# Attention of the latent feed-forward block: values of two head pairs at once on four 32-column tiles, one output bank, three banks in turn for the transposes

## The reference, cut to what matters

```python
ckv = x @ Wkva
kv_latent, k_rope = (ckv[:, :, :R], ckv[:, :, R:])            # R = 16
kv = (kv_latent @ Wkvb).reshape(b, t, H, NOPE).transpose(0, 2, 1, 3)
q = jnp.concatenate([q_nope, _rope(q_rope)], axis=-1)
k = jnp.concatenate([kv, _rope(k_rope)], axis=-1)
v = jnp.concatenate([kv, jnp.zeros_like(k_rope)], axis=-1)
att = jnp.einsum('bhqd,bhkd->bhqk', q, k) / jnp.sqrt(jnp.float32(D))
mask = jnp.tril(jnp.ones((t, t), dtype=bool))
att = jnp.where(mask, att, jnp.float32(-jnp.inf))
att = jax.nn.softmax(att, axis=-1)
y = jnp.einsum('bhqk,bhkd->bhqd', att, v)
return y.transpose(0, 2, 1, 3).reshape(b, t, H * D) @ Wo
```

## Time and profile before

| what | value |
| --- | --- |
| median of 3 runs | 2208.24 us (2206.58 to 2211.63) |
| the profiled execution | 2207.7 us |
| its span in the profile | 2205.9 us |
| loop of `attention_2f`, first scores to last values, each of four | 75.1 us (first: 459.3 to 534.4) |
| PE busy over the span | 1917.1 us, 87% |
| DVE, ACT, POOL busy | 55%, 42%, 36% |
| mean granted TensorE clock | 0.925 of full speed |

### The profile page before, as it was taken

One profiled execution on the slowest core, in us unless ns is written; L12 is line 12 of the kernel. 1 busy time (PEld: TensorE's weight loads), 2 busy tenths in 40 slices (PEclk: granted clock), 3 DMA queues, 4 the chain that ended last, 5 costly groups with the idle time before them and its releaser, 6 DMA issues. The chain is left out here.

```text
span 2205.9 us, 32131 instructions
## 1 busy us (share of the span) xinstructions
PE 1917.1 (87%) x11205; PEld 1234.1 (56%) x11205; DVE 1217.5 (55%) x3078; ACT 925.5 (42%) x2062; POOL 797.5 (36%) x959
## 2 busy tenths in 40 slices
PE   3369799898969989989896999989897998979989
PEld 3236556555655646656574655656574565646655
DVE  4336746455476636546386645646466464654544
ACT  0025355344543436527353336526453552542221
POOL 0124536454351116545252014635343453530000
PEclk9569899999989999989897999999898999999999
DMA  5120000001102000000203000000200000030030
GB/s 188 45 84 1 0 1 1 1 1 32 47 16 107 1 5 1 1 1 1 77 1 122 1 5 1 1 1 1 78 1 1 1 1 1 1 111 5 2 118 5
DMA packets 32303, 59.08 MB, mean 27 GB/s; under 512 B 6160, under 2 KB 10512, under 8 KB 30992
## 3 DMA queue, kind: packets, MB, share of 16 engines
q1 hardware_dynamic: 32144, 57.03, 7.3%
HBM read 53.86 MB, written 3.16 MB: 26 GB/s over the span
## 5 line engine op out<-in xcount | busy, mean ns | idle before, releaser
L1213 POOL TENSOR_TENSOR rows<-rows,rinv 128x512 f32<-128x512 f32 x256 | 260.7, 1039 | 311.2 <-DVE rinv L1398 311.2
L1393 DVE TENSOR_REDUCE nmax<-psum 128x2 f32<-128x1088 f32 x128 | 165.1, 1290 | 124.4 <-PE psum L1263 124.4
L1354 ACT ACTIVATE rows<-psum,nmax 128x544 f32<-128x544 f32 x256 | 180.3, 709 | 52.0 <-DVE nmax L1393 52.0
L1988 ACT ACTIVATE region_b<-psum 128x512 f32<-128x512 f32 x132 | 78.8, 597 | 256.4 <-PE psum L1933 256.3
L2029 DVE TENSOR_TENSOR region_b<-region_b,psum 128x512 f32<-128x512 f32 x128 | 87.9, 686 | 160.9 <-PE psum L1957 154.0
L1273 PE MATMUL psum<-weights,rows 128*128 128x128 f32 x1024 | 162.5, 281 | 7.2 <-ACT turned L1361 3.7
L1257 PE MATMUL psum<-region_a,region_b 64*128 64x256 f32 x1024 | 160.2, 404 | 9.7 <-ACT rows L1354 5.9
L1957 PEld LDWEIGHTS psum<-region_c,region_b 128*128 128x128 f32 x1024 | 133.7, 192 | 47.6 <-issue 27.9
L1273 PEld LDWEIGHTS psum<-weights,rows 128*128 128x128 f32 x1024 | 114.8, 148 | 58.7 <-issue 58.7
L1291 PE MATMUL psum<-turned,region_a 128*64 128x256 f32 x1024 | 137.9, 391 | 3.8 <-DVE turned L1404 3.5
L1404 DVE COPY turned<-psum 128x512 f32<-128x512 f32 x128 | 88.5, 691 | 87.9 <-PE psum L1273 87.7
(11 more groups left out here) (468 smaller groups left out, 3804.3 us busy)
## 6 DMA issues: line engine op xcount, KB each, us to landing
region_a<-w_centred SPq DMA_DIRECT2D x32, 258.0 KB, 5.3
region_a<-in_w SPq DMA_DIRECT2D x32, 256.0 KB, 4.6
region_a<-in_eg SPq DMA_DIRECT2D x32, 256.0 KB, 5.7
region_a<-in_eu SPq DMA_DIRECT2D x32, 256.0 KB, 5.9
region_c<-in_weights SPq DMA_DIRECT2D x32, 256.0 KB, 6.7
weights<-in_weights SPq DMA_DIRECT2D x4, 1264.5 KB, 9.3
w_centred<-region_a SPq DMA_DIRECT2D x1, 2064.0 KB, 6.3
region_a<-in_w SPq DMA_DIRECT2D x1, 2048.0 KB, 22.3
```

The source lines that it names most:

```text
L1213: nc.gpsimd.tensor_tensor(row, row, rinv[:, 2 * u + j:2 * u + j + 1].broadcast_to([P, S]), ALU.mult).then_inc(done, 1)
L1354: nc.scalar.activation(heads_of(u, j), scores_of(u, j), ACT.Exp, bias=nmax[:, 2 * u + j:2 * u + j + 1], accum_out=psum_of[:, 2 * u + j:2 * ...
L1393: nc.vector.tensor_reduce(nmax[:, 2 * u:2 * u + 2], both_scores(u), AX.X, ALU.max, negate=True).then_inc(s.mx, 1)
```

## The change

`values` works on a group of two pairs: for each of the four key blocks it issues four products (two pairs, two heads), each on a 32-column tile of its own, so that all four column tiles of the array have work. It runs at the steps 11, 19, 27 and 35 instead of 7, 11, 15, ..., 35, four times in place of eight, with the same number of matmuls altogether. All groups write bank 7 and each waits for the copy of the group before it. Bank 6, now free, joins 4 and 5: transposes take the three in turn. The transposed rows of three pairs are kept instead of two; the third pair's lie in the unused halves of `region_c` (first head) and `turned` (second head).

```diff
+            def turned_head(p, j):
+                if p % 3 < 2:
+                    return turned_f[:, 2 * (p % 3) + j, :, :]
+                return part(region_c if j == 0 else turned, T * S, [P, T, S])
+
             def turned_to(u, j):
-                p, t = u // T, u % T
-                return turned_f[:, 2 * (p % 2) + j, 0:t + 1, P * t:P * (t + 1)]
-
-            def o_bank(p):
-                return bank(6 + p // 2 % 2)
+                t = u % T
+                return turned_head(u // T, j)[:, 0:t + 1, P * t:P * (t + 1)]
+
+            def turn_bank(u, j):
+                return bank(4 + (2 * u + j) % 3)
...
                     def turn(u, j):
                         pe.wait_ge(s.pn, u + 1)
-                        if u >= 1:
-                            pe.wait_ge(s.ca if j == 0 else s.cb, u)
+                        if j == 0 and u >= 2:
+                            pe.wait_ge(s.cb, u - 1)
+                        if j == 1 and u >= 1:
+                            pe.wait_ge(s.ca, u)
                         for k in range(u % T + 1):
-                            mm = nc.tensor.transpose(bank(4 + j)[:, P * k:P * (k + 1)], rows_of(u)[:, j, P * k:P * (k + 1)],
+                            mm = nc.tensor.transpose(turn_bank(u, j)[:, P * k:P * (k + 1)], rows_of(u)[:, j, P * k:P * (k + 1)],
                                                      ident[:, :])
...
-                    def values(p):
-                        pe.wait_ge(s.ca, T * (p + 1))
-                        pe.wait_ge(s.cb, T * (p + 1))
-                        if p >= 4 and p % 2 == 0:
-                            pe.wait_ge(s.on, p // 2 - 1)
+                    def values(g):
+                        pe.wait_ge(s.ca, 2 * T * (g + 1))
+                        pe.wait_ge(s.cb, 2 * T * (g + 1))
+                        if g >= 1:
+                            pe.wait_ge(s.on, g)
                         for k in range(T):
-                            for j in range(2):
-                                lo = 2 * LAT * (2 * (p % 2) + j)
-                                mm = nc.tensor.matmul(o_bank(p)[lo:lo + 2 * LAT, P * k:S], latv[:, k, :],
-                                                      turned_f[:, 2 * (p % 2) + j, k, P * k:S],
+                            for n in range(4):
+                                lo = 2 * LAT * n
+                                mm = nc.tensor.matmul(bank(7)[lo:lo + 2 * LAT, P * k:S], latv[:, k, :],
+                                                      turned_head(2 * g + n // 2, n % 2)[:, k, P * k:S],
                                                       start=(k == 0), stop=(k == T - 1), skip_group_check=True)
                         mm.then_inc(s.o, 1)
...
-                        if step >= 7 and step % T == 3:
-                            values(step // T - 1)
+                        if step >= 11 and step % (2 * T) == 3:
+                            values(step // (2 * T) - 1)
...
                     def copy_first(u):
                         act.wait_ge(s.ta, u + 1)
-                        if u >= 2 * T:
-                            act.wait_ge(s.o, u // T - 1)
+                        if u >= 3 * T:
+                            act.wait_ge(s.o, (u // T - 3) // 2 + 1)
...
                     def copy_heads(g):
-                        act.wait_ge(s.o, 2 * (g + 1))
-                        nc.scalar.activation(aot[:, g, :], bank(6 + g % 2), ACT.Copy).then_inc(s.on, 1)
+                        act.wait_ge(s.o, g + 1)
+                        nc.scalar.activation(aot[:, g, :], bank(7), ACT.Copy).then_inc(s.on, 1)
...
                     def copy_second(u):
                         dve.wait_ge(s.tb, u + 1)
-                        if u >= 2 * T:
-                            dve.wait_ge(s.o, u // T - 1)
+                        if u >= 3 * T:
+                            dve.wait_ge(s.o, (u // T - 3) // 2 + 1)
```

More of the change, by code:

```diff
@@ L1580, in copy_first @@
                         act.wait_ge(s.ta, u + 1)
-                        if u >= 2 * T:
-                            act.wait_ge(s.o, u // T - 1)
-                        nc.scalar.activation(turned_to(u, 0), bank(4)[:, 0:keys(u)].rearrange("p (k q) -> p k q", q=P),
+                        if u >= 3 * T:
+                            act.wait_ge(s.o, (u // T - 3) // 2 + 1)
+                        nc.scalar.activation(turned_to(u, 0), turn_bank(u, 0)[:, 0:keys(u)].rearrange("p (k q) -> p k q", q=P),
                                              ACT.Copy).then_inc(s.ca, 1)
                     def copy_heads(g):
-                        act.wait_ge(s.o, 2 * (g + 1))
-                        nc.scalar.activation(aot[:, g, :], bank(6 + g % 2), ACT.Copy).then_inc(s.on, 1)
+                        act.wait_ge(s.o, g + 1)
+                        nc.scalar.activation(aot[:, g, :], bank(7), ACT.Copy).then_inc(s.on, 1)
                     for step in range(units + 4):
@@ L1620, in copy_second @@
                         dve.wait_ge(s.tb, u + 1)
-                        if u >= 2 * T:
-                            dve.wait_ge(s.o, u // T - 1)
-                        nc.vector.tensor_copy(turned_to(u, 1), bank(5)[:, 0:keys(u)].rearrange("p (k q) -> p k q", q=P)).then_inc(s.cb, 1)
+                        if u >= 3 * T:
+                            dve.wait_ge(s.o, (u // T - 3) // 2 + 1)
+                        nc.vector.tensor_copy(turned_to(u, 1), turn_bank(u, 1)[:, 0:keys(u)].rearrange("p (k q) -> p k q", q=P)).then_inc(s.cb, 1)
                     for step in range(units + LAG + 1):
```

## The result

The changed kernel takes 2228.84 us (median of 4 runs, 2226.4 to 2233.4) against 2209.59 (2206.58 to 2211.63): a ratio of 1.0091, 95% interval 1.0070 to 1.0112, 19 to 20 us slower. The forecast was 2229.

What follows compares the result with a forecast made beforehand. The prediction took alternating ACT and DVE work, 8.32 us a pair, as the bound, not PE. Terms -0.2 + 3.0 + 2.7 = +5.5 us an execution, +22 for four, on 2207.7, put at 2229 us; range 2206 to 2242.

Steps and rivals of the forecast that it cites:

- ACT and DVE are the bound, PE is as long beside them: Loop of attention_2f: ACT and DVE take turns, 8.32 us a pair; PE takes 8.34 but does not set the pace.
- the ring: Loop of attention_2f: row maximum (DVE), exponentials (ACT), reciprocals (DVE), next maximum, each waiting for the last; 8.32 us a pair.
- Four tiles run side by side: Values on PE: a group of two pairs takes 2.28 instead of 4.56 us, freeing 9.1 us of PE an execution.
- The tiles-in-turn rival: Values on PE: third and fourth tile run after the first two, 4.56 us a group, +36 us, 2243; chance 0.09.
- The head's 0.2 us: Start of the loop: the first values move away and the maximum at 477.91 gains 0.17 us; 0.2 us an execution.
- Banks and waits cost and gain nothing: Transposes, copies and bank 7: the new waits are long satisfied if the tiles run together; worth nothing in the steady part.
- Idle PE brings half clock: PE stretches left without values: idleness drops the granted clock to half rate, at 1.0 us for each such stretch.
- The inner falls, 3.0 us a loop: Units 7, 15 and 23, pairs without values: all three bring half clock at 1.0 us each; bounds 0 and 3.
- The tail, 2.7 us: Loop's end: half clock slows unit 31's transposes by 0.9 us and values by 1.8; bounds 0 and 6.7 us.
- The sum: Whole kernel: -0.2 + 3.0 + 2.7 = +5.5 us an execution, +22 us for four; bounds -0.8 and about +38.
- the clock that stays up: Rival for PE's clock: it stays up or falls once at no cost, 2207 to 2212 us; chance 0.24.

Runs made afterwards that it cites:

- cutting the ring: Kernel before the change with two DVE lines exchanged, row maximum of unit u issued ahead of the reciprocals of unit u-1: 2201.82 us, ratio 0.9958.
- the kernel with the banks alone: Kernel before with values pair by pair on two tiles, but one output bank (7), three turn banks and the three-pair buffer: 2212.51 us, ratio 1.0005.
- the exchange and all its fills: Changed kernel with row maximum ahead of reciprocals, redundant products at steps 31, 32, 33 and eight instructions at each of 7, 15, 23: 2200.91 us, ratio 0.9954.

## Why the prediction was right

- *ACT and DVE are the bound, PE is as long beside them.* Right, and shown: with some 9 us of PE's work a loop taken away the pairs stay at 8.32 to 8.42 us where the clock stayed up, and cutting the ring made PE the bound at 8.34. The ring of 8.32 holds for every second pair; in the others, which have the copy of the output bank in ACT's list, it is 8.41 or 8.42.
- *Four tiles run side by side.* Right: 32 instructions in 2.36 us, as the last row above shows, against 16 in 2.35. The Trainium skill (TensorE: Matmul & The Clock Gate, Part 3: Packing small matmuls) has 2.38 times for three tiles, of 3 that could be had, so not quite the "nearly all" of the prediction. Here four give twice the work of two in the same time. The tiles-in-turn rival is out.
- *The head's 0.2 us.* Right: its second pair takes 8.32 instead of 8.55 us. It is the only gain that the loops show.
- *Banks and waits cost and gain nothing.* Right within 0.25%, by the kernel with the banks alone.
- *Idle PE brings half clock.* Right, and shown by taking it away: with the holes filled by useless work the ratio is 0.9995. The Trainium skill (TensorE: Matmul & The Clock Gate, Part 1) says that activity releases the throttle. These traces agree: more work in the same holes kept the clock at 1.00. The longest single wait in the costly hole shown above was 1.65 us.
- *The inner falls, 3.0 us a loop.* This is the term of the sum that was mis-sized. The price was near (9.17 + 8.73 against 8.32 + 8.42 is 1.2 us a fall, forecast 1.0), but I let all twelve holes bring one, and three did, 0.9 us a loop. Four, four and six of twelve did in the three other kernels that have these holes open and the old order of DVE. "The new stretches are as thin as that one, in the same place of the pair" was true and not enough.
- *The tail, 2.7 us.* Right: 2.2 in the first loop, 2.8 to 3.0 in the others. Its parts fit too: the transposes lose 0.88 us (1.97 against 1.09, forecast 0.9), the values 1.4 to 2.1 (3.72 to 4.50 against 2.36, forecast 1.8).
- *The sum.* +5.5 a loop was forecast, +3.3 came in the loops of the one profile. That the total is nevertheless within 0.2 us is partly luck, in two ways. The forecast added 22 us to a profiled execution of 2207.7; measured are 19 to 20 us over a median of 2209.6, so two deviations cancel. (The sum as written ends at 2230.2 with the 0.5 for the median, and was put down as 2229.) And of the rise outside the loops 1.7 us are the one projection at half clock, which was in the bound of the tail; the rest lies in blocks that the change doesn't touch. Why these are longer is open: they have falls of the clock of their own, ahead of the first loop too, and one profile of each kernel can't tell a shifted start from chance.
- *A slip.* The rival that lies within 0.2% of no change is the first of the list, the clock that stays up, not the second.

## What to carry to other kernels

When the busiest engine has no idle time, look for a ring of others with the same period before taking work from it: here two bounds of 8.34 and 8.32 us lay on top of each other. Less work for PE alone lost 0.9%, the cut ring alone gained 0.4%, most of it at the head. Work taken from PE off the critical path is not free: in these traces the thinner stretch can halve the clock for the work behind it. And look first at the order in which an engine's instructions are written; two lines exchanged gave the 0.4%, as much as the changed kernel reached with the exchange and all its fills.

## What the runs showed of the hardware that was not expected

- Two holes alike to 0.03 us of PE's busy time (1.24 and 1.27 us of 3.40) had different ends: 1.00 and half clock. A fill of 2.35 us that ended 3.2 us ahead of the last transposes lost its effect in three of four loops; where it ended 2.95 us ahead, with the inner holes filled too, it had its effect in all four. What decides was not tried.
- Four streams of float32 columns into four column tiles cost no more than two: 2.36 against 2.35 us.
- The 64 useless instructions a loop cost no time that shows (loops of 75.2 or 75.3 us, against 75.3 before), and they gave back 20 us.
